# Order of two steps in an attention and feed-forward kernel on eight cores: products with V one head later, and the next pair's quantizing chain ahead of a down projection

## What is computed

```python
# attention: window of 128 to both sides, token 0 sees all and is seen by all
x = x + layernorm(attn(layernorm(x), Wq, Wk, Wv, Wo))
scores = where(mask, einsum('bnsd,bntd->bnst', q, k) * 64 ** -0.5, -inf)
out = einsum('bnst,bntd->bnsd', softmax(scores), v)

# feed-forward with quantized activations (8 bit a row) and ternary weights
def bitlinear(x, w):
    return einsum('bsi,oi->bso', act_quant(x), weight_quant(w))
x = x + layernorm(bitlinear(silu(bitlinear(h, w_gate)) * bitlinear(h, w_up), w_down))
# h = layernorm(x); act_quant: scale 127 / max|x| of the row, round, scale back
```

## Time and profile before

| | us |
|---|---|
| median of 4 runs | 8042.26 |
| lowest and highest run | 7951.36 and 8136.07 |
| profiled execution, its own time | 7954.59 |
| its span, slowest core (core 3) | 7952.7 |
| spans of the eight cores | 7926.1 to 7952.7 |
| PE busy, of the span | 5553.5 (70%) |
| VectorE (DVE) busy | 3723.5 (47%) |
| ScalarE (ACT) busy | 2488.9 (31%) |

### The profile page before, as it was taken

One profiled execution on the slowest core, in us unless ns is written; L12 is line 12 of the kernel. 1 busy time (PEld: TensorE's weight loads), 2 busy tenths in 40 slices (PEclk: granted clock), 3 DMA queues, 4 the chain that ended last, 5 costly groups with the idle time before them and its releaser, 6 DMA issues. The chain is left out here.

```text
span 7952.7 us, 120317 instructions; the slowest of 8 cores (7926.1 to 7952.7 us)
## 1 busy us (share of the span) xinstructions
PE 5553.5 (70%) x34578; PEld 2978.7 (37%) x34578; DVE 3723.5 (47%) x8559; ACT 2488.9 (31%) x3778; POOL 92.0 (1%) x184
## 2 busy tenths in 40 slices
PE   3665676666666666556537887877877877877877
PEld 2433343443433344333323333333333333333333
DVE  4555544545554454555434444444444444444443
ACT  0123332234232251332413323323333333333333
POOL 1000000000000000000000000000000000000000
PEclk9766666665667657666558988988988988988988
DMA  3111111112111111111362322322322322322321
GB/s 102 33 48 47 43 30 38 35 38 57 45 38 42 35 40 26 45 44 48 88 196 75 96 83 74 96 83 75 96 83 75 96 83 75 96 82 75 96 81 64
DMA packets 450183, 536.23 MB, mean 67 GB/s; under 512 B 112672, under 2 KB 374816, under 8 KB 448544
## 3 DMA queue, kind: packets, MB, share of 16 engines
q1 hardware_dynamic: 407552, 427.86, 17.6%
q0 software_dynamic: 18432, 33.56, 2.8%
q10 hardware_dynamic: 23584, 67.12, 2.2%
HBM read 486.54 MB, written 75.50 MB: 71 GB/s over the span
## 5 line engine op out<-in xcount | busy, mean ns | idle before, releaser
L1374 PE MATMUL PA<-wd_sb,hqT 128*128 128x512 bf16 x4096 | 1079.5, 417 | 0.0
L71 ACT ACTIVATE Asb<-PC,cm 128x512 bf16<-128x512 f32 x608 | 417.8, 687 | 1154.0 <-PE PC L665 1142.0
L1374 PEld LDWEIGHTS PA<-wd_sb,hqT 128*128 128x128 bf16 x4096 | 418.4, 106 | 471.1 <-issue 137.8
L1163 PE MATMUL PE<-wgsl,xqT 128*128 128x512 bf16 x2048 | 537.6, 410 | 37.2 <-DMA wd_sb<-wdTd 36.7
L704 PE MATMUL PE<-Vt,Asb 128*128 128x65 bf16 x1920 | 180.9, 235 | 531.0 <-DVE Asb L71 524.7
L1171 PE MATMUL PF<-wu_sb,xqT 128*128 128x512 bf16 x2048 | 508.0, 393 | 0.0
L71 ACT ACTIVATE Asb<-PD,cm 128x512 bf16<-128x512 f32 x608 | 417.7, 687 | 250.2 <-PE PD L665 220.1
L71 DVE SCALAR_TENSOR_TENSOR Hb<-gs_sb,statsC,PF 128x512 bf16<-128x512 bf16 x256 | 191.4, 748 | 638.5 <-PE PF L1171 633.2
L71 DVE TENSOR_TENSOR Asb<-Asb,M_MID 128x512 bf16<-128x512 bf16 x832 | 354.2, 426 | 279.9 <-ACT Asb L71 238.0
L1171 PE MATMUL PB<-wu_sb,xqT 128*128 128x512 bf16 x2048 | 483.8, 379 | 0.0
L1163 PE MATMUL PB<-wgsl,xqT 128*128 128x512 bf16 x2048 | 483.8, 379 | 0.0
(11 more groups left out here) (187 smaller groups left out, 8278.5 us busy)
## 6 DMA issues: line engine op xcount, KB each, us to landing
wgsl<-wgTd SPq DMA_DIRECT2D x256, 1024.0 KB, 5.3
wld<-wg SPq DMA_DIRECT2D x64, 512.0 KB, 4.1
wld<-wu SPq DMA_DIRECT2D x64, 512.0 KB, 4.1
wld<-wd SPq DMA_DIRECT2D x64, 512.0 KB, 4.4
y<-out_sb ACTq DMA_DIRECT2D x64, 512.0 KB, 2.8
xt<-x POOLq DMA_DIRECT2D x64, 256.0 KB, 5.1
xr<-x POOLq DMA_DIRECT2D x64, 256.0 KB, 4.5
x1d<-x1sl ACTq DMA_DIRECT2D x64, 256.0 KB, 2.0
```

What stands on the lines that cost most here:

```text
L71: instr = real(*a, **k)
L1163: last = self.e.matmul(self.ppsum(gp), h.xqT[i][:, 128 * kc:128 * (kc + 1)], h.wgsl[(kwg - 1) % 2][:, 512 * kc:512 * (kc + 1)], start=(kc ...
L1374: last = self.e.matmul(h.psum[pooldown][:, 512 * half:512 * (half + 1)], h.hqT[sl2][:, 128 * j:128 * (j + 1)], h.wd_sb[:, 1024 * icj + 512 ...
```

## The change

Two edits, each of the order alone. In a2_heads, for the blocks of four key blocks, pend becomes a list of two heads: the product with V is emitted after the scores of the next two heads, and after the last head two products follow. In phase_B, b_quant_chain_b of the next pair is called before bdown_body of tile 0 rather than after it. No instruction is added or removed.

```diff
         if nt == 4:
-            pend = None
+            pend = []
             for hh in range(NH):
                 ghead = self.tick("ghead")
                 aslots = scores_part(hh, ghead, [0])
                 self.caps[("vm", ghead)] = self.t["vMask"]
-                if pend is not None:
-                    av_part(*pend)
-                pend = (hh, ghead, aslots)
-            av_part(*pend)
+                if len(pend) == 2:
+                    av_part(*pend.pop(0))
+                pend.append((hh, ghead, aslots))
+            for p in pend:
+                av_part(*p)
         else:
@@
             def _head1():
                 hold["k1"] = self.bdown_head_s(sg, 1, kvh1)
 
-            self.bdown_body(sg, 0, SGT * sg, hold["k0"], headfn=_head1)
             if sg + 1 < NSG:
                 self.b_quant_chain_b(sg + 1)
+            self.bdown_body(sg, 0, SGT * sg, hold["k0"], headfn=_head1)
             self.bdown_body(sg, 1, SGT * sg + 1, hold["k1"])
```

## The result

The changed kernel takes 3.0% longer: the ratio of its time to the kernel before is 1.0295, 95% interval 1.0175 to 1.0414. That excludes no change, but the lower end is under the 2% that the prediction took as the least that can be told. The median of seven runs is 8420 us (8183 to 8556), of the kernel before over the ten runs now known 8129 us. Both medians hold executions in which the cores of one die had a lower clock, and the ratio leaves these out; the three of the seven without it took 8183, 8201 and 8245 us. The profiled execution of the changed kernel took 8201 us, 246 us more than that of the kernel before (7955).

What follows compares the result with a forecast made beforehand. The prediction took latencies to bound the head loop and in-order waits the feed-forward stage; 7954.6 + 489 - 186 = 8258 us, or 8345 against the median, so 8300 us, range 8190 to 8430.

Steps and rivals of the forecast that it cites:

- the bounds: Feed-forward loss of 489 us: 529 if the table load can't hide, 446 if 1.3 us more return in the pause.
- Start of tile 0's body: Feed-forward stage: the first hqT eviction waits for the second tile's statistics and comes 18.4 us later in each pair.
- The pause: Between a pair's two bodies: Ln and Exp (1.36 us) and the table load (1.28 us) go, 2.64 us back.
- The rest of the pair: Feed-forward stage: body 0 keeps its 19.13 us and VectorE's moved work costs nothing; net loss 15.78 us a pair.
- Head loop: Attention: VectorE becomes the bound at 1.19 us a head instead of 1.40; 3.1 us a block, 186 us gained.
- The bound for catching on each other's buffers: Head loop: VectorE and TensorE, nearly equal, hold each other up at 1.30 us a head; gain only 90 us.
- The hidden wait: Rival at tile 0's body: statistics are ready, the moved Ln costs nothing; 7687 us, not more than 2 in 100.
- The full clock in attention: Rival: TensorE gets its full clock in attention, projections gain 173 us; 8085 us, 8 in 100 for this or enough.
- The unmoved loop: Rival: late-freed buffers keep the head loop at 1.40 us a head, only the loss is left; 8444 us, 6 in 100.

Runs made afterwards that it cites:

- e3: Changed kernel with only the first tile's Ln and Exp of the next pair ahead of tile 0's body, the rest of the chain behind it; own time 8082 us.
- e5: e4 with the x1 loads behind the weight slices of the first two steps and the statistics in steps 3 to 7; own time 7710 us.
- e6: Head-loop edit alone, plus the next pair's four ACTIVATEs moved between d_sb of tile 0 and ScalarE's wait for its statistics; own time 7733 us.
- e2: Kernel before with only the chain edit (next pair's chain ahead of tile 0's body), head loop as before; own time 8375 us, ratio 1.0529.
- e7: e6 with the rest of each body's tail (d_sb statistics, Ln and Exp, output, store) emitted later; own time 7304 us.
- e8: Head-loop edit alone, plus a second equal RECIPROCAL on VectorE in each head of the four-key-block blocks; own time 7983 us.
- e9: Kernel before, plus a second equal RECIPROCAL on VectorE in each head of the four-key-block blocks; own time 7998 us.
- e11: e7 with the next pair's four ACTIVATEs moved behind the third eviction of tile 1's body; own time 7132 us, ratio to the kernel before 0.9037.
- e4: Changed kernel with VectorE's next-pair statistics spread over gate and up steps 2 to 7, x1 tiles loaded at step 1; own time 7920 us.

## Why the prediction was right, point by point

The direction, the range and the mechanism held: 8420 us in 8190 to 8430. The predicted 8300 us stood midway between two readings, the profiled execution's (8258) and the median's (8345). The execution took 8201, 57 us under the first; the median of the runs came 75 us over the second. Each lies within 11 us of an end of the range, and that the median did is partly luck: the median of the kernel before itself went from 8042 to 8129 us with six more runs, and the range was built on the first. The mechanism doesn't rest on that. Against the execution's own time the sum was 489 - 186 = +303 us, and +246 was measured: the feed-forward stage lost 444 us for 489, attention gained 197 for 186. (In the bounds 15.78 - 1.3 is 14.48 and not 14.4 us a pair, 449 us for 446; nothing hangs on it.)

- **Start of tile 0's body.** Predicted 18.42 us a pair, measured 18.42 on the median (19.29 - 0.87). e3 and e5 show that it is the wait for the statistics and nothing else: with half of the wait the eviction came 12.53 us later, with none 2.64.
- **The pause.** Predicted 2.64 us back, measured 2.63. The table load went with the four ACTIVATEs. In e6 the load begins 0.08 us after the read of the accumulator before it ends, and Ln 1.29 us after that, so the load's own 1283 ns are the price here. The Trainium skill (ScalarE: Activation LUTs, section What ACT_TABLE_LOAD costs) adds a drain of about 1.38 us to every switch of tables; the trace doesn't agree, since by it an estimated 5.8 us of pause would have been left, and 7.19 was measured.
- **The rest of the pair.** Predicted nothing, measured 1.6 us less a pair on the mean, 50 us over 31 pairs, and this is the mis-sized step: "a longer idle time has little to take away". It gave something, so that a pair got 14.3 us longer and not 15.8. On medians, body 0 took 17.8 us for 19.2, body 1 0.6 longer, the gate steps and the next start 0.7 and 0.6 shorter. The clock differs in the first 6.92 us of body 0 (the first row is of the kernel before, the second of the changed one; length, engines, clock):

```profile
5985.88:5992.80 6.92, 6.92 (x29) 3.20 (x30) 5.75 (x13) 2.01 (x3) 0.00 (x0) 0.59 0.00 0
```

```profile
6422.37:6429.29 6.92, 6.92 (x35) 3.35 (x36) 3.91 (x19) 2.71 (x4) 0.00 (x0) 0.79 0.01 2
```

TensorE was granted 0.59 of its clock there before and 0.79 after, having idled 3 us before and 21.7 after. Over 6.92 us that is 1.4 us of clock, and the body is 1.3 us shorter. The same sum goes for both bodies, in both kernels and in e2, e3, e5 and e7, over 30 pairs each: a body's length less the clock that it lost (its length times one minus the granted share) is 15.7 to 16.2 us every time. So the bodies differ by the clock. The length of the idle time alone doesn't set it: in e2 the same body takes 17.8 us, in e3 (15.6 us of idle time) 19.0, in e5 (5.8 us) 18.75, and in the changed kernel, behind 21.4 to 21.9 us of idle time in every pair, it took from 17.6 to 19.3 us. Four of its 30 bodies took over 19 us; the first 6.92 us of one of them:

```profile
7491.02:7497.94 6.92, 6.91 (x26) 3.09 (x27) 3.86 (x18) 2.02 (x3) 0.00 (x0) 0.57 0.01 2
```

Why the full clock returned sooner in most pairs after the longer wait, and where the 0.7 and 0.6 us of the gate steps and the next start come from, no run settles; I leave it open.
- **Head loop.** Predicted 3.1 us a block and 186 us; the span from first to last product fell by 3.24 us (21.07 to 17.83 on the mean of 60), from first scores to the AO transposes by 3.21, and the stage by 197. VectorE sets it: 1.19 us from mask to mask, and e8 against e9 shows that it does so only now. The bound for catching on each other's buffers (90 us) wasn't needed: products do wait for AO, 206 us in all, but VectorE loses nothing by it.
- **The rivals.** The hidden wait: the statistics end 18.5 us behind the start of the last Silu in both kernels; e5 shows what it takes to hide it, and that the gain imagined for it was too large, since the four ACTIVATEs then stand in front of the first eviction (2.64 us, not free). The full clock in attention didn't come: the mean clock to 3900 us is 0.68 in both kernels. The unmoved loop is refuted.

## What to carry to other kernels

An instruction that is moved ahead is priced by what its wait holds back on its own engine, not by its own 0.2 us: 1.4 us of ACTIVATEs cost 18.4 us a pair, since an in-order ScalarE had all of TensorE's evictions behind them. Before moving a producer's consumer, find the first place in that engine's timeline that is idle and where the input is ready; here it lay behind d_sb, and further on behind the first evictions of the next tile. Where a loop is one of latencies (its period is a sum over engines, none of them full), one more stage of distance between production and use gains down to the busiest engine's own time, and a second stage gains next to nothing (here under 30 us).

## What the runs showed that I had not expected

- Body 0 ran faster on the median after 21.5 us of idle time than after 3.1 us (17.8 and 19.2 us), by an earlier return of the full clock: 0.79 for 0.59 of it in the first 6.9 us of the bodies shown. In four of 30 pairs it didn't.
- In e11 the body of tile 1 took 16.4 us in 20 of 30 pairs, at a granted clock of 1.00 throughout, and 18.0 in the ten others (at 0.91), where it had been 18.3 in the kernel before with a pause of 9.8 us and not 1.4. On the mean, 16.9 us, it gained 1.6 us on e7, so that the pair gained 4.4 us where 2.6 had been moved. The row above, at 5502 us, is of one of the ten.
- In e4 two loads of 256 KB, moved ahead of two weight slices on the transfer queue, cost 5.9 us a pair (last d_sb to first Silu 19.87 us, 13.95 in e5) through the wait that one of them carried.
